# Other written-out orders for both phases of a fused scan and local-attention kernel

## The chip, the cores and the metric

One Trainium2 chip, one of its cores. The metric is the device time of one execution in microseconds (us). Two numbers are compared: the time before the change and the time after it, each the median of several runs.

## The reference, cut to what matters

Sixteen sequences of 512 tokens of width 256 pass through two blocks, each behind a layer norm, a modulation by a condition vector and a gated residual. The first is a selective scan (512 channels, 16 states each), the second two layers of windowed attention with a gated feed-forward part.

```python
h = _layernorm(x) * (1 + ca) + sa
xz = einsum(h, W_in);  x_ssm, z = split(xz)
dt = softplus(x_ssm @ W_dt + b_dt);  B_mat, C_mat = x_ssm @ W_B, x_ssm @ W_C
# for each token: h = exp(dt * A) * h + dt * B * x;  y = sum over states of h * C
y = (y + x_ssm * D) * silu(z)
x = x + ga * (y @ W_out)
h = _layernorm(x) * (1 + cb) + sb
for l in range(2):                       # 8 heads of 64, windows of 128 tokens
    q, k, v = split(shift_token(h) @ wqkv[l])
    q, k = rotary_xpos(l2norm(q) * qs, l2norm(k) * ksc)
    h = h + local_attention(q, k, v) @ wo[l]
    a, g = split(layernorm(shift_token(h)) @ w1[l] + b1[l])
    h = h + (a * gelu(g)) @ w2[l] + b2[l]
x = x + gb * h
```

## The kernel before, in words

The kernel runs two phases one after the other, `mixer_pass` (the scan block) and `stack_pass` (the two attention layers). Each is a software pipeline written in the same way. The work of one sequence is cut into named steps, such as `scan:7`. One long string, `MIXER_ORDER` (L139 to L160) or `ORDER` (L829 to L838), lists all steps of one pass, and every engine executes those steps of the list that it has a part in, in the order of the list, once per pass. The engines meet only at semaphores, so what matters is the order on each engine, not where a step of one engine stands against one of another. Each step has a lead, the sequence that it works on against the number of the pass; a "-" behind the name lowers it by one, a "+" raises it by one. So a pass holds work of three sequences. The scan phase works through 16 sequences, the second phase through 32 (16 in each of two layers), each with a filling pass ahead and a draining one behind.

**Scan phase.** The 512 channels x 16 states of a sequence are 32 units of 128 channels x 2 states x 512 tokens. Of unit q, `bcast:q` (TensorE, L565) spreads B over the partitions into one of two PSUM slots, `mul:q` (VectorE, L737) multiplies it by the step's input u, `decay:q` (ScalarE, L684) computes the decays, `scan:q` (VectorE, L755) runs the recurrence, `cmul:q` (GpSimd, L813) multiplies by C, and `sum:q` (TensorE, L573) adds the states up in PSUM. For ten of the units `mul` is GpSimd's (L806) and the decays go into the PSUM slot. `gate:d` (VectorE, L761) closes a chunk of 128 channels; gate 2 needs sums 0 to 30 and gate 3 sum 31. The slot of `bcast:q` is free when `scan:q-2` is done. `dtadd` (GpSimd, L792, L796) makes u for half of the channels. Decays, the rows of C and of B that are loaded from DRAM, and the states live in rings of 3, 2, 2 and 6 buffers (L33). A second set of TensorE steps makes the inputs of the next sequence: `xT`, `hT` (transposes), `xs`, `z`, `bc`, `dt` (projections, L524), and `out`, `mean2`, `var2` (L492) end the previous one.

**Second phase.** On TensorE: `pq`, `pk`, `v` (projections of one window of 128 tokens, L1296), `ptr` (transposes of rotated q and k, L1326), `score` (L1346), `pt` (transposes of the probabilities, L1357), `att` (L1373), `wo` (L1286), `mean`, `var`, `ga:0` to `ga:5` (the two halves g and a of the feed-forward part, 128 hidden columns each, 6 matmuls per half, L1407; `ga:5` has a g alone) and `wd:0` to `wd:5` (L1428). On ScalarE: `psq` (squares of q and k, L1459), `prate` (L1466, L1468), `exp` (eight heads, L1506), `gelu` (L1557), `hh` (L1571), `ptc` (copy of the transposed q out of PSUM, L1474), `dev`, `hn` and copies. On VectorE: `pss` (L1669, L1673), `pnorm` (L1680), `prot` (by sine, L1695), `padd` (L1701), `mask` (L1728, L1734), `rate` (L1745), `gated` (L1802), `hns` (cuts the normalised tokens in two parts for TensorE, L1650, L1652). On GpSimd: `prot` (by cosine, L1601), `pn` (L1628), `hl` (L1635).

A string `BANK_OF` gives each product of TensorE one of the eight PSUM banks; before a product starts, TensorE waits until the bank's last product has been read (`Banks.wait_free`). The bank of g0 to g4 is read out by `gelu`, that of a0 to a4 by `gated`, of q_t by `ptc` on ScalarE. ScalarE changes its function table between `gelu` and the exponentials, so a `gelu` that is followed by an `exp`, `prate` or `dev` in the list has a table load behind it (`LAST_GELUS`), and the next `gelu` one ahead of it. Squares of q and k are written to the buffer `qk_rot`, which later takes the rotated ones; `square_qk` waits for the sums of the squares of the window before, and since TensorE's order has `ptr:w-1` ahead of `pq:w`, the transposes have read the buffer by then.

Of the kernel before, what the change touches and what calls it, by code (L numbers as in the profile page):

```python
# [32 lines left out]
DECAY_SLOTS, STATE_SLOTS, C_SLOTS, B_SLOTS = 3, 6, 2, 2  # L33
# [106 lines left out]
sum-:5 bcast-:10 sum-:6 mul-:12 mul-:13 xload:0 bcast-:11 scan-:12 cload-:13 cload-:14 cload-:15 scan-:13 cload:0  # L140
cload:1 bload:6 sum-:7 cmul-:10 cload:2 mul-:14 sum-:8 cload:3 decay-:18 bcmid-:0 xs-:0 cmul-:11 cmul-:12 cmul-:13
cmul-:14 xscopy-:3 cload:4 decay-:19 cload:5 bcast-:12 sum-:9 decay-:20 xs-:1 xs-:2 decay-:21 mul-:15 scan-:14
scan-:15 mul-:16 cload:6 scan-:16 bload:9 mul-:17 bcast-:13 bcrest-:0 decay-:22 cmul-:15 mul-:18 soft-:0 scan-:17
decay-:23 bcast-:14 bcast-:15 mul-:19 cload:7 cload:8 gate-:0 bclow-:0 gate-:1 cmul-:16 cmul-:17 decay-:24 zcopy-:0
cmul-:18 cmul-:19 cmul-:20 decay-:25 sum-:10 zcopy-:1 cstore:0 sum-:11 bc-:0 bcast-:16 scan-:18 zcopy-:2 decay-:26
decay-:27 cload:9 sum-:12 zcopy-:3 decay-:28 bload:12 scan-:19 bcast-:17 cload:10 decay-:29 cmul-:21 sum-:13 mul-:20
mul-:21 soft-:1 scan-:20 xs-:3 sum-:14 bcast-:18 scan-:21 decay-:30 mul-:22 mul-:23 sum-:15 mul-:24 mul-:25 dt-:0
cmul-:22 decay-:31 scan-:22 bcast-:19 bcast-:20 decay:0 skip-:1 scan-:23 decay:1 stat:0 cload:11 bcast-:21
scan-:24 sum-:16 sum-:17 cmul-:23 bcast-:22 sum-:18 bcast-:23 decay:2 sum-:19 scan-:25 decay:3 cmul-:24 sum-:20
sum-:21 mul-:26 mul-:27 dtadd-:0 z-:0 scan-:26 decay:4 bcast-:24 scan-:27 x1store:0 silu-:0 z-:1 mul-:28 decay:5  # L150
cload:12 bcast-:25 z-:2 mul-:29 bcast-:26 z-:3 scan-:28 cmul-:25 cmul-:26 cmul-:27 norm:0 cmul-:28 cmul-:29 bcast-:27
h2store:0 sum-:22 dt-:1 cmul-:30 bcast-:28 scan-:29 sum-:23 bcast-:29 mul-:30 sum-:24 mul-:31 sum-:25 xcopy:0 decay:6
# [710 lines left out]
def stack_pass(nc, inp, mod, x1_dram, stack_dram, parts_dram, rotary_dram, out):  # L863
# [5 lines left out]
    with ExitStack() as ctx:  # L869
# [17 lines left out]
        mask = squares[:, 2:4, :].rearrange("p a b -> p (a b)")  # L887
# [565 lines left out]
        def _(act):  # L1453
            def square_qk(s, slot, layer, w):
                for i, stem in enumerate("qk"):
                    psum.wait_full(act, s, f"{stem}{w}")
                    if i == 0:
                        act.wait_ge(qk_sum_done.sem, qk_sum_done.at(s, w))
# [187 lines left out]
        def _(dve):  # L1646
# [38 lines left out]
            def times_sin(s, slot, layer, w):  # L1685
# [3 lines left out]
                if s == 0:  # L1689
                    dve.wait_ge(rotary_done, 1)  # L1690
# [347 lines left out]
```

## Time and profile before

| what | value |
|---|---|
| time, median of 3 runs | 4316.37 us (4315.1 to 4318.74) |
| the profiled execution's own time | 4316.54 us |
| its span | 4314.5 us |
| TensorE (PE) busy | 4052.9 us, 94% |
| VectorE (DVE) busy | 3679.9 us, 85% |
| ScalarE (ACT) busy | 2672.4 us, 62% |
| GpSimd (POOL) busy | 2639.3 us, 61% |
| granted TensorE clock, mean | 0.981 |

The scan phase fills the first 1.74 ms of the span, the second phase the rest. The page gives shares over the whole span; since the two phases have different limits, each has to be read from its own stretch. PE is TensorE's matmuls, PEld its weight loads, which run beside them. A line "A <- B: t, n" of the waits says that A stood idle for t us in n waits, which B ended.

### The profile page before, as it was taken

What the parts mean: (1) busy time and instruction counts of PE and PEld (TensorE: products, weight loads), DVE (VectorE), ACT (ScalarE), POOL (GpSimd) and SP (SyncE); (2) the same over time, 40 slices, a digit from 0 to 9 for tenths busy, and PEclk for the clock granted to TensorE, in tenths of its full rate; (3) what the DMA queues carried; (4) which work ended last, traced back from release to release, by engine and by line L of the source; (5) the groups of instructions that cost most, each with busy time, mean ns of one, the idle gap of its engine ahead of it and who ended that gap; (6) DMA issues with size and microseconds to landing.
All of it is one profiled execution on the core that took longest, in us unless ns stands there. A gap on an engine that the chain in (4) does not pass through costs nothing.

```text
span 4314.5 us, 60081 instructions
## 1 busy us (share of the span) xinstructions
PE 4052.9 (94%) x19614; PEld 2629.3 (61%) x19614; DVE 3679.9 (85%) x5981; ACT 2672.4 (62%) x5767; POOL 2639.3 (61%) x1297
## 2 busy tenths in 40 slices
PE   7999999999999999659999999999999999999997
PEld 4444444444444444347777777777777777777775
DVE  4999999999999999668888788888888888888873
ACT  5666666666666665335656565665656566565654
POOL 3999999999999999553434434343434334343432
PEclk8999999999999999879999999999999999999998
DMA  2333333333333333421000000001010100101000
GB/s 96 108 118 121 123 120 118 118 118 119 122 118 118 121 121 112 144 78 35 16 27 19 26 21 25 21 17 63 29 68 21 35 26 27 33 25 35 20 30 25
DMA packets 118499, 295.02 MB, mean 68 GB/s; under 512 B 21208, under 2 KB 43664, under 8 KB 118192
## 3 DMA queue, kind: packets, MB, share of 16 engines
q1 hardware_dynamic: 116320, 291.15, 20.2%
q8 instruction: 160, 2.62, 0.3%
q14 instruction: 147, 1.20, 0.1%
q10 hardware_dynamic: 1872, 0.05, 0.0%
HBM read 248.52 MB, written 42.64 MB: 67 GB/s over the span
## 4 chain that ended last, share of the span: by engine, by line
PE 34%; DVE 14%; issue 4%; ACT 4%; DMA 1%; SPq 0%; POOL 0%; DVEq 0%; ACTq 0%
PE b_bank L1407 12%; PE b_bank L1428 6%; PE b_bank L1296 5%; PE b_bank L1357 3%; PE b_bank L1373 3%; PE b_bank L1286 3%; ACT b_scores L1506 2%; DVE b_scores L1728 2%; DVE b_qk L1680 2%; DVE b_qk_rate L1669 2%; PE b_bank L1326 1%; PE b_bank L1346 1%; DVE b_qk_rot L1695 1%; DVE b_qk_rot L1701 1%; DVE b_xc L1785 1%
## 5 line engine op out<-in xcount | busy, mean ns | idle before, releaser
L813 POOL TENSOR_TENSOR a_state<-a_state,a_c_wide 128x1024 f32<-128x1024 f32 x512 | 1196.0, 2369 | 37.4 <-DVE a_state L755 37.4
L1628 POOL TENSOR_TENSOR b_scores<-b_scores,b_row_rate 128x1024 f32<-128x1024 f32 (+1 forms) x256 | 426.5, 1682 | 969.6 <-DVE b_row_rate L1745 969.6
L573 PE MATMUL a_y_sum<-a_state,a_ident 128*128 128x512 f32 x2048 | 942.3, 598 | 0.7 <-POOL a_state L813 0.6
L755 DVE TENSOR_TENSOR_SCAN a_state<-a_decay,a_slot 128x1024 f32<-128x1024 f32 x352 | 788.9, 2271 | 1.9 <-ACT a_decay L684 0.6
L1296 PE MATMUL b_bank<-b_w_qkv,b_hx_part 128*128 128x512 f32 x2304 | 661.7, 426 | 35.2 <-DVE b_w_qkv L1830 16.2
L1506 ACT ACTIVATE b_scores<-b_scores,b_row_bias 128x256 f32<-128x256 f32 (+1 forms) x1024 | 478.0, 469 | 269.9 <-DVE b_row_bias L1734 269.9
L573 PEld LDWEIGHTS a_y_sum<-a_state,a_ident 128*128 128x128 f32 x2048 | 387.1, 191 | 401.0 <-issue 342.4
L684 ACT ACTIVATE a_decay<-a_dt,a_neg_a 128x512 f32<-128x512 f32 x704 | 458.8, 711 | 164.0 <-DVE a_state L755 163.8
L1407 PE MATMUL b_bank<-b_hn_part,b_w 128*128 128x512 f32 x2112 | 515.4, 399 | 25.6 <-DVE b_hn_part L1652 25.6
L1296 PEld LDWEIGHTS b_bank<-b_w_qkv,b_hx_part 128*128 128x128 f32 x2304 | 424.0, 193 | 157.7 <-issue 48.2
L1601 POOL TENSOR_TENSOR b_by_cos<-b_qk,b_rotary 128x1024 f32<-128x1024 f32 x128 | 336.7, 2631 | 252.0 <-DVE b_qk L1680 249.9
L1407 PEld LDWEIGHTS b_bank<-b_hn_part,b_w 128*128 128x128 f32 x2112 | 397.4, 189 | 134.4 <-DVE b_hn_part L1652 40.8
L737 DVE TENSOR_TENSOR a_slot<-a_u,a_slot 128x1024 f32<-128x1024 f32 x352 | 417.2, 1213 | 24.6 <-PE a_slot L565 24.5
L806 POOL TENSOR_TENSOR a_state<-a_u,a_b_wide 128x1024 f32<-128x1024 f32 x160 | 375.9, 2369 | 27.6 <-PE a_y_sum L573 26.4
L684 ACT ACTIVATE a_slot<-a_dt,a_neg_a 128x512 f32<-128x512 f32 x320 | 208.0, 682 | 273.1 <-DVE a_state L755 272.4
L1635 POOL TENSOR_TENSOR b_h_part<-b_h,b_h_part 128x512 fp32r<-128x512 f32 x160 | 205.2, 1291 | 267.9 <-ACT b_h_part L1571 267.9
L755 DVE TENSOR_TENSOR_SCAN a_state<-a_slot,a_state 128x1024 f32<-128x1024 f32 x160 | 357.9, 2269 | 6.7 <-ACT a_slot L684 6.4
L1728 DVE CUSTOM_DVE_ANT_0 b_scores<-b_bank,b_squares 128x256 f32<-128x256 f32 (+1 forms) x1024 | 337.5, 385 | 3.4 <-issue 3.4
L1428 PE MATMUL b_bank<-b_h_part,b_w 128*128 128x512 f32 x1088 | 296.2, 406 | 0.0
L1802 DVE SCALAR_TENSOR_TENSOR b_h<-b_bank,b_b_1a,b_gelu 128x512 f32<-128x512 f32 x192 | 143.4, 747 | 167.5 <-POOL b_h_part L1635 64.3
L565 PE MATMUL a_slot<-a_bc_parts,a_picks 96*128 96x512 bf16 x704 | 213.4, 386 | 69.0 <-DVE a_state L755 67.6
L1357 PE MATMUL b_bank<-b_squares,b_scores 128*128 128x128 f32 x1792 | 265.2, 277 | 12.3 <-DVE b_qk L1680 7.9
(201 smaller groups left out, 6859.4 us busy)
## 6 DMA issues: line engine op xcount, KB each, us to landing
a_c_wide<-bc_rows SPq DMA_DIRECT2D x256, 512.0 KB, 3.7
a_b_wide<-bc_rows SPq DMA_DIRECT2D x80, 512.0 KB, 4.8
b_hx<-stack_rows SPq DMA_DIRECT2D x64, 256.0 KB, 3.6
b_x_res<-stack_rows SPq DMA_DIRECT2D x32, 512.0 KB, 3.3
a_xt<-in_L_attn_x SPq DMA_DIRECT2D x16, 512.0 KB, 6.2
x_rows<-a_x_t SPq DMA_DIRECT2D x16, 512.0 KB, 5.3
stack_rows<-a_h_t SPq DMA_DIRECT2D x16, 512.0 KB, 5.3
stack_rows<-b_xc SPq DMA_DIRECT2D x16, 512.0 KB, 2.6
```

Of the source, the lines that this page charges most:

```text
L573: last = nc.tensor.matmul(y_sum[dd][:], ident[:], state[state_ring.slot[q]][:, i, :], start=False, stop=(j == GROUPS - 1 and i == GROUP - 1))
L684: last = nc.scalar.activation(to[:, i, :], dt[slot][:, d, :], ACT.Exp, scale=neg_a[:, d, n:n + 1])
L737: nc.vector.tensor_tensor(slots[q % 2][:], u[slot][:, d, :].unsqueeze(1).to_broadcast([P, GROUP, SEQ]), slots[q % 2][:], ALU.mult).then_in ...
L755: nc.vector.tensor_tensor_scan(flat(h), flat(factor), flat(term), 0.0, ALU.mult, ALU.add).then_inc(scan_done.sem, 1)
L813: nc.gpsimd.tensor_tensor(h[:], h[:], c_wide[c_ring.slot[q // 2]][:], ALU.mult).then_inc(cmul_done.sem, 1)
L1296: last = nc.tensor.matmul(psum.tile(name)[:], x[:, c, w * P:(w + 1) * P].bitcast(F32R), weights[:, c, cols:cols + INNER].bitcast(F32R), st ...
L1357: last = nc.tensor.transpose(psum.tile(name)[:, n * P:(n + 1) * P], scores[w % 2][:, h, blk * WINDOW:(blk + 1) * WINDOW], ident)
L1407: last = nc.tensor.matmul(psum.tile(f"{stem}{m}")[:], weights[:, c, at * P:(at + 1) * P].bitcast(F32R), x[:, c, :].bitcast(F32R), start=(n ...
L1428: last = nc.tensor.matmul(psum.tile(f"wd{m}")[:], weights[:, k, m * P:(m + 1) * P].bitcast(F32R), x[:, held, :].bitcast(F32R), start=(k == ...
L1506: e = nc.scalar.activation(scores[w % 2][:, h, lo:hi], scores[w % 2][:, h, lo:hi], ACT.Exp, bias=row_bias[:, w, h:h + 1], accum_out=row_su ...
L1628: nc.gpsimd.tensor_tensor(probs, probs, row_rate[:, w, at].unsqueeze(2).to_broadcast([P, 4, hi - lo]), ALU.mult)\
L1728: last = nc.vector.tensor_tensor_reduce(out=scores[w % 2][:, head, lo:hi], in0=psum.tile(f"s{w}_{g}_{h}")[:, at + lo:at + hi], in1=mask[:, ...
```

## The change

The change replaces both order strings and the table of banks, enlarges three rings of the scan phase (decays 3 to 4, rows of C 2 to 3, rows of B 2 to 3), and puts the squares of q and k into the buffer `qk` of the normalised ones. For this `square_qk` waits for both readers of `qk` in the window before, `times_sin` waits until the transposes of the window before have read `qk_rot`, and `normalise_qk` loses a wait. Every step is there as often as before. The diff, with the scan phase's string cut to the lines around the end of a sequence:

```diff
-DECAY_SLOTS, STATE_SLOTS, C_SLOTS, B_SLOTS = 3, 6, 2, 2
+DECAY_SLOTS, STATE_SLOTS, C_SLOTS, B_SLOTS = 4, 6, 3, 3
...
-cload:12 bcast-:25 z-:2 mul-:29 bcast-:26 z-:3 scan-:28 cmul-:25 cmul-:26 cmul-:27 norm:0 cmul-:28 cmul-:29 bcast-:27
-bcast-:30 scan-:30 bcast-:31 sq2:0 sum-:26 sum-:27 scan-:31 bload+:1 mul:0 sum-:28 decay:7 mul:1 bcast:0 bcast:1
-sum-:29 dev2:0 cmul-:31 decay:8 bcast:2 gate-:2 scan:0 mul:2 gate-:3 scan:1 xcopy:1 scan:2 scan:3 decay:9
-mul:3 mul:4 res:0 sum-:30 mod:0 cmul:0 scan:4 sum-:31 skip:0 decay:10 out:0 bcast:3 res:1 cmul:1 bcast:4 mul:5 out:1
-sum:1 cmul:5 mul:7 scan:6 bcast:7 mul:8 scan:7 xn2:0 decay:13 bload+:4 scan:8 xscopy:0 sum:2 decay:14 decay:15
-decay:16 xscopy:1 h2:0 scan:9 mul:9 xscopy:2 bcast:8 cmul:6 var2:0 bccopy:0 mul:10 xT:1 hcut:0 mul:11 cmul:7 cmul:8
...
+mul-:27 cmul-:27 scan-:26 scan-:27 decay:8 sum-:24 bcast-:29 mul-:28 sum-:25 mul-:29 sum-:26 bcast-:30 mod:1 up:1
+sum-:27 scan-:28 bcast-:31 cload:7 scan-:29 dt-:1 mul-:30 sum-:28 cload:8 bcast:0 dtadd-:0 sum-:29 bcast:1 mul-:31
+sum-:30 decay:9 cmul-:28 scan-:30 cload:9 scan-:31 cmul-:29 sum-:31 bload:12 decay:10 decay:11 cmul-:30 dev2:0 mul:0
+skip:0 scan:0 mul:1 xcopy:1 out:0 bcast:2 gate-:2 gate-:3 xscopy:0 scan:1 decay:12 bcast:3 cload:10 scan:2 h2store:0
+cmul-:31 scan:3 sum:0 mul:2 res:0 bcast:4 bcast:5 out:1 mul:3 decay:13 cmul:0 sum:1 mul:4 cmul:1 h2:0 mean2:0 mul:5
+bcast:6 xscopy:1 decay:14 dtadd-:1 cmul:2 cmul:3 scan:4 decay:15 xT:0 cstore:0 bcast:7 bcast:8 res:1 scan:5 cen2:0
...
-ptr-:3 mask:0.0 mask:0.1 att-:3 score:0.0 exp:0 pn:0.0 hxs:0 hxload:0 psq:0 score:0.1 score:1.0 wo:0 mask:1.0 add:0
-prate:0 rate:0 pss:0 pnorm:0 pq:0 pk:0 pn:0.1 resload:0 score:1.1 mask:1.1 add:1 prot:0 score:2.0 exp:1 padd:0 wo:1
-pn:1.0 rate:1 v:0 pt:0.0 pt:0.1 cen:0 vc:0 ptc:0 sq:0 psq:1 mean:0 pk:1 ptr:0 pn:1.1 mask:2.0 sqs:0 pq:1 pt:1.0 v:1
-prate:1 pss:1 pt:1.1 vc:1 dev:0 pnorm:1 var:0 mask:2.1 score:2.1 pt:1.2 v:2 pt:1.3 pk:2 prot:1 xn:0 att:0 onorm:0
-att:1 padd:1 mask:3.0 score:3.0 vc:2 hn:0 exp:2 hns:0 gelu:0 score:3.1 onorm:1 psq:2 mask:3.1 ptr:1 gated:0 rate:2
-pq:2 ga:0 pn:2.0 pss:2 ga:1 ptc:1 pn:2.1 hh:0 gated:1 gelu:1 prate:2 hl:0 pnorm:2 ga:2 ga:3 exp:3 gelu:2 pt:2.0 prot:2
-gated:2 pk:3 gated:3 hh:1 gated:4 ga:4 padd:2 hh:2 rate:3 pt:2.1 wd:0 x1load:0 gelu:3 gelu:4 hh:3 gelu:5 gated:5 ga:5
-ptc:2 ptr:2 pss:3 outstore:0 psq:3 pq:3 wd:1 pt:2.2 hl:1 wd:2 hh:4 prate:3 pnorm:3 hl:2 hl:3 pn:3.0 hh:5 hl:4 pt:2.3
-wd:3 pt:3.0 wd:4 hl:5 vc:3 pn:3.1 pt:3.1 fin:0 fin:1 wd:5 pt:3.2 prot:3 sum:0 sum:1 turnc:0 padd:3 pt:3.3 turnc:1
-onorm:2 ptc:3 v:3 store:0 att:2 turn:0 turn:1 onorm:3
+ptc-:3 pn:0.1 ptr-:3 pt-:3.2 pt-:3.3 score:0.0 mask:0.0 score:0.1 mask:0.1 att-:3 onorm-:3 hxs:0 hxload:0 exp:0
+score:1.0 mask:1.0 psq:0 prate:0 rate:0 wo:0 pq:0 pk:0 add:0 pss:0 pnorm:0 pt:0.0 pk:1 pt:0.1 resload:0 vc:0 mask:1.1
+prot:0 pn:1.0 padd:0 v:0 score:1.1 exp:1 add:1 score:2.0 wo:1 rate:1 ptr:0 psq:1 pq:1 ptc:0 store:0 sq:0 prate:1 vc:1
+mask:2.0 mean:0 cen:0 pss:1 sqs:0 v:1 pt:1.0 v:2 pnorm:1 pn:1.1 pt:1.1 dev:0 var:0 score:2.1 mask:2.1 pt:1.2 pt:1.3
+xn:0 onorm:0 prot:1 onorm:1 padd:1 vc:2 hn:0 gelu:0 x1load:0 pk:2 mask:3.0 pn:2.0 exp:2 att:0 hns:0 att:1 psq:2 ptc:1
+score:3.0 score:3.1 prate:2 mask:3.1 pk:3 ptr:1 pq:2 rate:2 pss:2 hl:0 gated:0 pnorm:2 hh:0 ga:0 exp:3 pn:2.1 ga:1
+gelu:1 prot:2 ga:2 gelu:2 gelu:3 ga:3 gated:1 hh:1 pt:2.0 hl:1 hl:2 gated:2 hl:3 ga:4 gated:3 gelu:4 rate:3 pt:2.1
+hh:2 wd:0 padd:2 pn:3.0 hh:3 ga:5 gated:4 hl:4 gelu:5 wd:1 outstore:0 hh:4 gated:5 ptc:2 ptr:2 pss:3 pq:3 hl:5 psq:3
+wd:2 pnorm:3 hh:5 pt:2.2 wd:3 pt:2.3 fin:0 wd:4 prate:3 fin:1 wd:5 pt:3.0 turnc:0 turnc:1 vc:3 v:3 att:2 pn:3.1 prot:3
+sum:0 sum:1 pn+:0.0 turn:0 padd:3 onorm:2 turn:1 pt:3.1
 BANK_OF = """
-q_t3:4 k_t3:5 wo0:5 s0_0_0:1 s0_0_1:5 s0_1_0:0 s0_1_1:2 wo1:7 s1_0_0:6 s1_0_1:7 q0:2 k0:6 s1_1_0:3 s1_1_1:4 pt0_0:4
-v0:1 mean:3 pt0_1:7 v1:4 s2_0_0:5 s2_0_1:0 s2_1_0:7 s2_1_1:2 k1:6 var:0 q_t0:2 k_t0:4 q1:1 pt1_0:2 pt1_1:5 pt1_2:5
-v2:3 pt1_3:6 s3_0_0:5 s3_0_1:4 k2:7 s3_1_0:6 s3_1_1:3 o0:3 o1:0 q_t1:2 k_t1:1 q2:5 k3:7 pt2_0:5 pt2_1:6 pt2_2:6
-pt2_3:1 g0:4 a0:0 g1:3 a1:2 g2:4 a2:6 g3:0 a3:2 g4:1 a4:3 wd0:4 wd1:5 g5:1 q_t2:2 k_t2:3 q3:0 pt3_0:7 pt3_1:7 pt3_2:0
-pt3_3:3 o2:7 o3:6 v3:6 y0:5 y1:2
+q_t3:2 k_t3:7 wo0:2 s0_0_0:3 s0_0_1:2 s0_1_0:7 s0_1_1:4 wo1:7 s1_0_0:7 s1_0_1:3 q0:5 k0:4 s1_1_0:3 s1_1_1:5 pt0_0:0
+v0:1 mean:5 pt0_1:7 v1:7 s2_0_0:0 s2_0_1:1 s2_1_0:3 s2_1_1:7 k1:2 var:5 q_t0:3 k_t0:6 q1:4 pt1_0:0 pt1_1:1 pt1_2:0
+v2:6 pt1_3:4 s3_0_0:7 s3_0_1:5 k2:1 s3_1_0:4 s3_1_1:2 o0:0 o1:3 q_t1:3 k_t1:5 q2:7 k3:6 pt2_0:4 pt2_1:4 pt2_2:4
+pt2_3:2 g0:0 a0:5 g1:0 a1:2 g2:3 a2:5 g3:7 a3:1 g4:0 a4:5 wd0:0 wd1:3 g5:7 q_t2:1 k_t2:4 q3:7 pt3_0:6 pt3_1:0 pt3_2:5
+pt3_3:6 o2:7 o3:6 v3:4 y0:5 y1:6
...
-        qk_sq = qk_rot
+        qk_sq = qk
-                        act.wait_ge(qk_sum_done.sem, qk_sum_done.at(s, w))
+                        act.wait_ge(by_cos_done.sem, by_cos_done.at(s, w))
+                        act.wait_ge(by_sin_done.sem, by_sin_done.at(s, 2 * w))
-                dve.wait_ge(by_cos_done.sem, by_cos_done.at(s, w))
+                dve.wait_ge(k_t_full.sem, k_t_full.at(s, w))
```

Read engine by engine, the strings differ in these places, among others. Only steps of the engine named are shown, with "|" where a pass ends.

```
scan phase, VectorE   before: scan-:30 scan-:31 mul:0 mul:1 gate-:2 scan:0 gate-:3 scan:1 scan:2 scan:3
                      after:  scan-:30 scan-:31 mul:0 scan:0 mul:1 gate-:2 gate-:3 scan:1 scan:2 scan:3
scan phase, TensorE   before: z-:3 bcast-:27 sum-:22 dt-:1 bcast-:28 sum-:23 bcast-:29 sum-:24 sum-:25 bcast-:30
                              bcast-:31 sum-:26 sum-:27 sum-:28 bcast:0 bcast:1 sum-:29 sum-:30 sum-:31 skip:0 out:0
                      after:  z-:3 bcast-:27 sum-:22 sum-:23 bcast-:28 sum-:24 bcast-:29 sum-:25 sum-:26 bcast-:30
                              sum-:27 bcast-:31 dt-:1 sum-:28 bcast:0 sum-:29 bcast:1 sum-:30 sum-:31 skip:0 out:0
                      before: bcast:7 sum:2 var2:0 xT:1 sum:3 sum:4 hT:0 hT:1 |
                      after:  bcast:7 sum:2 hT:0 sum:3 hT:1 sum:4 sum:5 var2:0 bcast:10 sum:6 bcast:11 sum:7 | xT-:1
second phase, ScalarE before: dev:0 pt:1.2 vc:2 hn:0 exp:2 gelu:0 psq:2 ptc:1 hh:0 gelu:1 prate:2 exp:3 gelu:2
                      after:  dev:0 pt:1.2 vc:2 hn:0 gelu:0 exp:2 psq:2 ptc:1 prate:2 hh:0 exp:3 gelu:1 gelu:2
second phase, TensorE before: pk:2 att:0 att:1 score:3.0 score:3.1 ptr:1 pq:2 ga:0 ga:1 ga:2 ga:3 pt:2.0 pk:3 ga:4
                      after:  pk:2 att:0 att:1 score:3.0 score:3.1 pk:3 ptr:1 pq:2 ga:0 ga:1 ga:2 ga:3 pt:2.0 ga:4
second phase, VectorE before: mask:3.0 hns:0 onorm:1 mask:3.1 gated:0 rate:2 pss:2 ptc:1 gated:1 pnorm:2
                      after:  mask:3.0 hns:0 ptc:1 mask:3.1 rate:2 pss:2 gated:0 pnorm:2 prot:2 gated:1
```

## Rows read from the trace of the kernel before

**Rows 1.** By stretch: start:end, length, busy us (instructions) per engine, TensorE clock, DMA share, GB/s.
```profile
500.00:606.28 106.28, 100.15 (x300) 48.80 (x299) 103.64 (x67) 73.66 (x126) 102.78 (x48) 1.00 0.37 120
...
2508.28:2582.61 74.33, 73.53 (x457) 55.77 (x457) 61.36 (x152) 45.37 (x117) 30.02 (x17) 1.00 0.06 22
```
**Rows 2.** All waits of VectorE, and one of GpSimd, from 500 to 1600 us.
```profile
DVE a_u L761 <- PE a_y_sum L573: 18.1, 10, 1.9
DVE a_slot L737 <- PE a_slot L565: 6.2, 12, 1.4
DVE a_state L755 <- ACT a_slot L684: 2.7, 10, 0.3
...
POOL a_state L806 <- PE a_y_sum L573: 19.3, 17, 1.5
```
**Rows 3.** Timeline from 594 to 612 us: start, us, engine, what [idle before it].
```profile
596.97 4.46 DVE L755 TENSOR_TENSOR_SCAN a_state<-a_decay,a_slot 128x1024 f32<-128x1024 f32 x2
...
601.34 2.33 DVE L737 TENSOR_TENSOR a_slot<-a_u,a_slot 128x1024 f32<-128x1024 f32 x2
...
601.48 0.60 PE L565 MATMUL a_slot<-a_bc_parts,a_picks 96*128 96x512 bf16 x2 [0.43 <-DVE a_state L755]
...
601.92 5.32 PE L573 MATMUL a_y_sum<-a_state,a_ident 128*128 128x512 f32 x12
...
605.56 0.69 DVE L761 TENSOR_TENSOR a_u<-a_y_sum,a_sz 128x512 f32<-128x512 f32 x1 [1.89 <-PE a_y_sum L573]
```
**Rows 4.** TensorE's timeline in the second phase, from ga:0 on, one pass.
```profile
2582.61 11.46 PE L1407 MATMUL b_bank<-b_hn_part,b_w 128*128 128x512 f32 x48 [0.54 <-DVE b_hn_part L1652]
2593.90 0.60 PE L1357 MATMUL b_bank<-b_squares,b_scores 128*128 128x128 f32 x4
2594.26 1.63 PE L1296 MATMUL b_bank<-b_w_qkv,b_hx_part 128*128 128x512 f32 x6
```
**Rows 5.** ScalarE's timeline over the same stretch, exp:2 first.
```profile
2579.03 0.49 ACT L1506 ACTIVATE b_scores<-b_scores,b_row_bias 128x256 f32<-128x256 f32 x1
...
2583.07 1.28 ACT L1557 ACT_TABLE_LOAD   x1
2584.37 0.69 ACT L1557 ACTIVATE b_gelu<-b_bank,b_b_1g 128x512 f32<-128x512 f32 x1
2584.95 1.08 ACT L1459 ACTIVATE b_qk_rot<-b_bank 128x512 f32<-128x512 f32 x2
2585.91 0.61 ACT L1474 ACTIVATE b_q_t<-b_bank 128x512 f32<-128x512 f32 x1
2586.56 0.63 ACT L1571 ACTIVATE b_h_part<-b_h 128x512 fp32r<-128x512 f32 x1
2587.11 0.69 ACT L1557 ACTIVATE b_gelu<-b_bank,b_b_1g 128x512 f32<-128x512 f32 x1
2587.81 1.28 ACT L1560 ACT_TABLE_LOAD   x1
2589.11 0.22 ACT L1466 ACTIVATE b_qk_rate<-b_qk_rate 128x16 f32<-128x16 f32 x1
...
2589.57 0.49 ACT L1506 ACTIVATE b_scores<-b_scores,b_row_bias 128x256 f32<-128x256 f32 x1
```
**Rows 6.** VectorE's timeline over the same stretch.
```profile
2585.78 0.75 DVE L1802 SCALAR_TENSOR_TENSOR b_h<-b_bank,b_b_1a,b_gelu 128x512 f32<-128x512 f32 x1 [1.02 <-PE b_bank L1407]
...
2586.55 1.17 DVE L1669 TENSOR_REDUCE b_qk_rate<-b_qk_rot 128x16 f32<-128x1024 f32 x1
2587.75 0.88 DVE L1673 TENSOR_SCALAR b_qk_rate<-b_qk_rate 128x16 f32<-128x16 f32 x1
...
2606.81 0.17 DVE L1673 TENSOR_SCALAR b_qk_rate<-b_qk_rate 128x16 f32<-128x16 f32 x1
```
**Rows 7.** TensorE's timeline near the end of the span.
```profile
4224.84 13.02 PE L1407 MATMUL b_bank<-b_hn_part,b_w 128*128 128x512 f32 x48 [2.57 <-DVE b_hn_part L1652]
```
**Rows 8.** The same place by stretch, columns as in the first group.
```profile
4225.00:4232.00 7.00, 7.00 (x24) 5.54 (x25) 2.80 (x14) 3.52 (x5) 1.50 (x1) 0.76 0.00 0
```

More of the change, by code:

```diff
@@ L139 @@
 MIXER_ORDER = """
[L140 to L149, printed above, removed]
@@ L155 @@
-mul:3 mul:4 res:0 sum-:30 mod:0 cmul:0 scan:4 sum-:31 skip:0 decay:10 out:0 bcast:3 res:1 cmul:1 bcast:4 mul:5 out:1
-dtadd-:1 sum:0 bcast:5 up:0 cmul:2 scan:5 xT:0 bcast:6 mod:1 cen2:0 decay:11 up:1 cmul:3 cmul:4 mean2:0 decay:12 mul:6
-sum:1 cmul:5 mul:7 scan:6 bcast:7 mul:8 scan:7 xn2:0 decay:13 bload+:4 scan:8 xscopy:0 sum:2 decay:14 decay:15
-decay:16 xscopy:1 h2:0 scan:9 mul:9 xscopy:2 bcast:8 cmul:6 var2:0 bccopy:0 mul:10 xT:1 hcut:0 mul:11 cmul:7 cmul:8
-sum:3 cmul:9 sum:4 hcut:1 scan:10 scan:11 bcast:9 hT:0 decay:17 bcup:0 hT:1
+scan-:10 scan-:11 cmul-:6 cmul-:7 scan-:12 scan-:13 bcast-:13 bcmid-:0 xT-:1 xs-:0 xscopy-:3 xs-:1 decay-:19 soft-:0
@@ new lines @@
+cmul-:8 sum-:8 decay-:20 cmul-:9 decay-:21 mul-:12 mul-:13 mul-:14 xs-:2 decay-:22 cmul-:10 decay-:23 decay-:24
+bcast-:14 mul-:15 cmul-:11 cmul-:12 sum-:9 scan-:14 bcast-:15 sum-:10 bload:6 zcopy-:0 bc-:0 bcast-:16 decay-:25
+cload-:15 sum-:11 xload:0 scan-:15 decay-:26 zcopy-:1 bcast-:17 zcopy-:2 cmul-:13 mul-:16 bcrest-:0 cload:0 sum-:12
+cmul-:14 sum-:13 cload:1 decay-:27 sum-:14 decay-:28 bcast-:18 cmul-:15 mul-:17 mul-:18 cload:2 xs-:3 decay-:29
+bload:9 sum-:15 bcast-:19 dt-:0 zcopy-:3 bcast-:20 cload:3 mul-:19 scan-:16 cmul-:16 skip-:1 decay-:30 bcast-:21
@@ new lines @@
+scan-:17 gate-:0 bclow-:0 scan-:18 cload:4 decay-:31 sum-:16 decay:0 sum-:17 bcast-:22 gate-:1 silu-:0 sum-:18
+cmul-:17 cmul-:18 scan-:19 mul-:20 bcast-:23 mul-:21 scan-:20 decay:1 soft-:1 scan-:21 mul-:22 sum-:19 bcast-:24
+decay:2 sum-:20 bcast-:25 decay:3 cmul-:19 cmul-:20 cload:5 z-:0 z-:1 cmul-:21 mul-:23 decay:4 stat:0 mul-:24 mul-:25
+decay:5 decay:6 scan-:22 norm:0 cmul-:22 scan-:23 xcopy:0 cmul-:23 sq2:0 cmul-:24 cmul-:25 sum-:21 z-:2 cmul-:26
+x1store:0 bcast-:26 decay:7 z-:3 mod:0 bcast-:27 sum-:22 scan-:24 scan-:25 up:0 mul-:26 sum-:23 cload:6 bcast-:28
@@ L160 @@
+bcast:6 xscopy:1 decay:14 dtadd-:1 cmul:2 cmul:3 scan:4 decay:15 xT:0 cstore:0 bcast:7 bcast:8 res:1 scan:5 cen2:0
+cload:11 sum:2 cmul:4 hT:0 mul:6 sum:3 cload:12 hT:1 mul:7 scan:6 hcut:0 cmul:5 sum:4 scan:7 xscopy:2 bccopy:0
+bload+:1 sum:5 bload+:4 decay:16 bcast:9 var2:0 bcast:10 cload:13 scan:8 sum:6 mul:8 scan:9 mul:9 mul:10 xn2:0 mul:11
+hcut:1 decay:17 bcast:11 cload:14 sum:7 bcup:0 decay:18 bcast:12
 """
```

2 lines of the change are left out of this document (removed).

## The prediction

> **What bounds the kernel now.** Busy time by stretch first. In the scan phase one sequence takes 106.28 us and three engines are nearly full: VectorE is busy for 103.6 us of it, GpSimd for 102.8, TensorE for 100.2. In the second phase one sequence takes 74.33 us, TensorE is busy for 73.5 of it, VectorE for 61.4, ScalarE for 45.4 [rows 1]. So the scan phase is VectorE's, with at most 2.6 us to gain per sequence, and the second phase TensorE's, with at most 0.8. Both are short of their bound by waits alone, since no step is added or removed. The waits come second. VectorE's in ten sequences of the scan phase sum to 18.1 + 6.2 + 2.7 = 27 us, and two thirds of them are the gate's wait for a sum of states [rows 2]. In the second phase TensorE waits once per sequence, 0.54 us, for the cut of the normalised tokens ahead of ga:0 [rows 4]. The timeline comes last, to walk the new orders through with measured durations: an order of TensorE that is nearly free of gaps can be spoilt much more than it can be improved.
>
> **Scan phase: the gate.** Count from the end of scan:31, which the next multiplication follows at once (601.34) [rows 3]. Before, TensorE has bcast:1 next, which had to wait for just this scan (601.48), and only then sums 29, 30, 31: twelve matmuls in 5.3 us, so 1.7 to 1.8 us a sum. VectorE does two multiplications (2.33 us), then stands for 1.89 us until sum 30 is in [rows 3]. After, sum 29 lies before bcast:1. TensorE is through with sum 30 at about 0.1 + 0.6 + 1.8 = 2.5 us and with sum 31 at about 4.3 us if GpSimd keeps up, and VectorE has a scan (half of 4.46 us, [rows 3]) more to do ahead of the gate, so it comes there at 2.33 + 2.2 = 4.6 us. The 1.89 us go. What is late next: gate 3, at 5.2 us, needs sum 31 with less than 1 us to spare.
>
> **Scan phase: the rest.** The move of dt-:1 (12 matmuls) from in front of bcast-:28 and bcast-:29 to behind bcast-:31 takes it out of the way of a multiplication that waited for bcast-:29 (most of the 6.2 us in ten sequences); behind it stand only sum 28 and bcast:0, which are not late. GpSimd's wait of 1.5 us for sum 3 ahead of mul:9 (19.3 us in ten sequences, [rows 2]) goes too, since two steps (var2, xT:1) leave TensorE's way. On the other side hcut:0 now comes 2.8 us earlier on VectorE and needs a longer row of ScalarE's steps (sq2, a decay, mod, up), and dev2 now stands behind three more decays. I allow 0.9 us of new waits. Sum: 27 / 10 = 2.7 us of waits, 0.9 stays or is new, and GpSimd is full at 102.8 us: about 1.6 us less a sequence, bounds 2.6 (VectorE without a wait) and -1.0 (hcut and xn2 a microsecond late each, which would eat the gain and more). Over 15 steady sequences: -24 us, from -39 to +15.
>
> **Rings.** No wait for a DMA is among GpSimd's in the scan phase, and ScalarE's waits for free decay buffers lie in its idle third (73.7 us busy of 106.28) [rows 1, 2]. More buffers take away no wait that anybody waits for: 0 us. If the cover were gone, ScalarE would first lose its 32.6 idle us per sequence, and what is left would be inside the bounds above. The new order of SP's loads puts x1store and h2store between loads of C; both wait for steps of VectorE and ScalarE that are over before the ring has room for the next load. 0 us.
>
> **Buffer of the squares.** It costs nothing and gives nothing. In the new order, too, ptr:w-1 stands ahead of pq:w on TensorE, and ptr follows padd, which follows both products with cosine and sine. So when q is full, everything that square_qk and times_sin newly wait for is done. Above and below: a semaphore wait that is already met, a few hundredths of a us.
>
> **Second phase: gelu:0 ahead of exp:2.** This is the large term. Count from the first matmul of ga:0 (2582.61 before), and take ScalarE's row of steps. gelu:0 starts at 2584.37, 1.76 us after it, since it needs g0. Before, exp:2 was done by then (2579.03 to 2583.07) and psq:2 and ptc:1 followed at once [rows 5]. After, exp:2 stands behind gelu:0, though its scores are ready 3.6 us ahead of ga:0 at the latest (2579.03): gelu:0 and the table load that now follows it (2587.11 to 2587.81 to 2589.11: 0.70 + 1.30) end at 3.76; exp:2 takes 4.04 (2579.03 to 2583.07), to 7.80; psq:2 0.96, to 8.76; ptc:1 0.61, to 9.4 [rows 5]. The new table of banks gives g2 the bank of q_t1 (3), which ptc:1 reads out. TensorE comes to g2 after four products of six matmuls, 24 x 11.46 / 48 = 5.73 us [rows 4]. Everything else of TensorE is queued behind g2. It waits 3.7 us.
>
> **The second wait of the same pass.** a2 has the bank of a0, free after gated:0, which now stands behind pss:2: psq:2 ends at 8.76, the sum of squares takes 1.20 (2586.55 to 2587.75), the floor 0.17, gated:0 0.75, so 10.9; g2 ends at 10.8: 0.1 us. Then prate:2 (0.46, beside gated:0), hh:0 (0.55), exp:3 (4.04) and a table load (1.30) stand ahead of gelu:1: 10.9 + 0.6 + 4.0 + 1.3 = 16.8, and gelu:1 is through at 17.5 [rows 5, 6]. g4 has the bank of g1 (0), which gelu:1 reads. TensorE is through with g2 to a3 at 10.9 + 4.3 = 15.2 and with pt:2.0 (0.36) at 15.6, and waits 1.9 us. From there on gated:1 and gated:2 (0.75 each) end at 19.0, just when a4 needs its bank. Walking on to wd:5 I find no further wait. Sum: 5.7 us a sequence, in the 31 passes that have a gelu of one sequence beside the exponentials of the next.
>
> **What the second phase gives back.** The wait of 0.54 us at ga:0: VectorE now does prot:0 and padd:0 ahead of the residual (ahead of the chain to hns:0), while TensorE has one projection less between wo:1 and ga:0 (pk:1 and v:0 go ahead of wo:1, pk:3 comes in, 24 x 11.46 / 48 / 4 = 1.4 us each). By my walk hns:0 is then in time. I take 0.5 us; bounds 0.8 (all of TensorE's idle time) and -1.0 (another order of short products with more gaps between them). Sum of the phase: 31 x (5.7 - 0.5) = +161 us. Bounds: 31 x (3.7 - 0.8) = +90 if only the first wait stands on the path, 31 x (5.7 + 1.0) = +208.
>
> **Sum.** The profiled execution took 4316.54 us, 0.17 above the median of the runs. 4316.5 - 24 + 161 = 4453.5. Filling and draining passes and the weights' setup keep their work: 0, within 5 us either way.
>
> **Rivals.**
> (a) *The clock falls in the gaps.* Near the end of the span TensorE stood for 2.57 us, and the 48 matmuls behind it took 13.02 us in place of 11.46 [rows 4, 7]; the granted clock over these 7 us was 0.76, a part of it at 1.2 instead of 2.4 GHz [rows 8]. That is 1.56 us a fall. The first gap, 3.7 us, would slow g2 to a3, and the second wait absorbs that: it ends by ScalarE's row, not TensorE's. A fall in the second gap, 1.9 us, would be paid in full: 31 x 1.56 = 48, so 4502 us. For it: the 2.57 us gap. Against it: that one came after a stretch with many small gaps, and here 60 us of work without one come first. [...]
> (b) *Only the first wait is on the path*, because exp:3 and gelu:1 run beside TensorE's work better than I have it: 4316.5 - 24 + 31 x 3.2 = 4392 us.
> (c) *More waits behind*: VectorE loses some 10 us to waiting per sequence, 61.4 + 10 of 79.5 us. If its backlog makes one more product late by 2 us, 62 us: 4515 us.
> (d) *The other side.* ScalarE's row does not reach TensorE. The place is g2: it decides whether 9.4 us of ScalarE's row fit under what TensorE has to do between the start of ga:0 and g2. That is 5.73 us as I read the order; with another 3.7 us of work there, or if exp:2 ran ahead of gelu:0 in fact, nothing is lost and the phase gives its 0.5 us: 4316.5 - 24 - 16 = 4276 us. For it: TensorE reaches 99% in the kernel before with an order of the same kind. Against it: queues run in order, and every duration of the row is measured.
> (e) *The change does nothing*, because both gains and losses hide: within 0.2%, about 8.6 us, which is what a measurement here can tell from no change.
>
> **How the numbers follow.** Forecast 0.50, (a) 0.15, (b) 0.13, (c) 0.10, (d) 0.10, (e) 0.02. The forecast's own range is 4425 to 4480. The range of 4375 to 4525 takes in (a), (b) and the smaller half of (c). Faster 0.10, within 0.2% 0.02, slower 0.88.
>
> **What would show it.** The second phase's sequence takes about 79.5 us against 74.33. Ahead of one g product in the middle of ga TensorE stands for 3.7 us, released by ScalarE's copy of q_t, and ahead of g4 for 1.9 us, released by gelu. exp:2 starts 3.8 us after ga:0, not before it. In the scan phase the sequence takes 104.7 us, and the gate's wait of 1.9 us is gone. TensorE's share in the second phase falls to some 93%. I am wrong if these waits are absent or end by another engine, or if the scan phase's sequence is above 106.28 us.

## The result and the profile after

The changed kernel takes 4413.35 us (median of 4 runs, 4411.63 to 4415.54), the one before in the same session 4316.72 us (4315.1 to 4318.74). The ratio is 1.0224, interval 1.0206 to 1.0242: 97 us slower. The profiled execution took 4411.63 us, its span is 4409.8 us.

The two phases went in opposite directions. From the start of the span to the first product ga:0 it is 1941.60 us in place of 1987.82, so the scan phase gave 46.2 us. (Before, VectorE still runs a scan at 1767 us, so the scan phase fills a little more than the 1.74 ms named ahead of the prediction.) From there to the end it is 2468.2 us in place of 2326.7, so the second phase lost 141.5 us.

Busy time by stretch, one steady sequence of each phase after, the counterpart of [rows 1] (us of the stretch, then busy us and count of TensorE, weight loads, VectorE, ScalarE and GpSimd, granted clock, DMA share, GB/s):
```profile
500.00:603.66 103.66, 100.09 (x300) 48.96 (x299) 103.33 (x67) 73.57 (x126) 102.72 (x47) 1.00 0.37 123
2573.94:2652.83 78.89, 73.80 (x457) 55.86 (x456) 58.75 (x152) 46.22 (x116) 30.27 (x17) 1.00 0.06 21
```
The scan sequence is 103.66 us and VectorE is busy for 103.33 of it: it waits for next to nothing now. The second phase's sequence is 78.89 us in place of 74.33, and TensorE's busy time has hardly moved (73.80, before 73.53). What was added is waiting. In the second of the two layers a sequence takes 0.9 us more both before and after (75.25 and 79.76 us); over the 29 steady passes of both layers the change adds 131.7 us, 4.54 a pass.

VectorE's and GpSimd's waits from 500 to 1600 us, the counterpart of [rows 2] (us in total, times, longest):
```profile
DVE a_slot L737 <- PE a_slot L565: 2.3, 10, 0.2
POOL a_state L813 <- DVE a_state L755: 5.6, 10, 0.6
POOL a_state L806 <- PE a_y_sum L573: 2.5, 11, 0.2
```
The 18.1 us for the gate and 2.7 us for decays have gone, and 6.2 have become 2.3.

TensorE's timeline over one pass of the second phase, the counterpart of [rows 4] (start, us, engine, what, [idle before it and who ended it]; the edit to the buffers moved the line numbers by one):
```profile
2573.94 5.76 PE L1407 MATMUL b_bank<-b_hn_part,b_w 128*128 128x512 f32 x24
2583.09 6.10 PE L1407 MATMUL b_bank<-b_hn_part,b_w 128*128 128x512 f32 x24 [3.38 <-ACT b_q_t L1475]
2589.02 0.60 PE L1357 MATMUL b_bank<-b_squares,b_scores 128*128 128x128 f32 x4
2591.33 3.10 PE L1407 MATMUL b_bank<-b_hn_part,b_w 128*128 128x512 f32 x12 [1.71 <-ACT b_gelu L1558]
```
ga:0 starts without a wait. After 24 matmuls TensorE stands at g2 for 3.38 us until ScalarE has copied q_t, and at g4 for 1.71 us until gelu:1 is through, 17.39 us after the start of ga:0. In between there is a third, short wait that the merged rows do not show as idle: the first matmul of a2 starts 0.37 us behind the one ahead of it (2584.72 against 2584.35), where its neighbours follow at 0.23 us. It comes 0.05 us after gated:0, which reads out the bank that a2 is to have, is through on VectorE:
```profile
2583.92 0.75 DVE L1803 SCALAR_TENSOR_TENSOR b_h<-b_bank,b_b_1a,b_gelu 128x512 f32<-128x512 f32 x1
```
That is 0.14 us. After the waits at g2 and a2 the second matmul follows the first one at 0.34 us, not 0.23. These two starts (0.1 us each) and the 0.14 us are the 0.34 us by which the 24 matmuls behind g2's wait take longer than the 24 ahead of it (6.10 and 5.76).

ScalarE over the same stretch, the counterpart of [rows 5]:
```profile
2575.54 0.69 ACT L1558 ACTIVATE b_gelu<-b_bank,b_b_1g 128x512 f32<-128x512 f32 x1 [6.13 <-PE b_bank L1407]
2576.25 1.28 ACT L1561 ACT_TABLE_LOAD   x1
2577.55 0.51 ACT L1507 ACTIVATE b_scores<-b_scores,b_row_bias 128x256 f32<-128x256 f32 x1
...
2581.50 1.05 ACT L1460 ACTIVATE b_qk<-b_bank 128x512 f32<-128x512 f32 x2
2582.45 0.58 ACT L1475 ACTIVATE b_q_t<-b_bank 128x512 f32<-128x512 f32 x1
...
2589.30 1.28 ACT L1558 ACT_TABLE_LOAD   x1
2590.59 1.27 ACT L1558 ACTIVATE b_gelu<-b_bank,b_b_1g 128x512 f32<-128x512 f32 x2
```
This is the row of the prediction: ScalarE stands for 6.13 us ahead of gelu:0, since the exponentials that were ready are queued behind it. exp:2 starts 3.61 us after ga:0 and the copy of q_t ends at 9.09; g2 starts at 9.15.

The passes are not all alike. The same place two passes earlier, TensorE's timeline:
```profile
2424.52 7.32 PE L1407 MATMUL b_bank<-b_hn_part,b_w 128*128 128x512 f32 x24 [3.39 <-ACT b_q_t L1475]
2432.76 3.11 PE L1407 MATMUL b_bank<-b_hn_part,b_w 128*128 128x512 f32 x12 [0.48 <-ACT b_gelu L1558]
```
And by stretch, columns as above (the value after the five engines is the granted clock), the 24 matmuls in this pass, in the one shown first, and in the pass between:
```profile
2424.52:2432.02 7.50, 7.50 (x28) 6.01 (x28) 6.38 (x7) 6.38 (x20) 5.89 (x4) 0.78 0.00 0
2583.09:2589.09 6.00, 6.00 (x25) 4.55 (x26) 5.93 (x7) 4.91 (x18) 4.39 (x4) 1.00 0.00 0
2503.78:2512.28 8.50, 8.49 (x26) 6.71 (x27) 6.67 (x8) 7.37 (x22) 6.89 (x4) 0.65 0.01 3
```
The wait at g2 comes in 30 passes. In 26 of them the 24 matmuls behind it take 7.2 to 8.7 us, and the granted clock is below 1.00: a part of them ran at 1.2 in place of 2.4 GHz. In the other four they take 6.10 us. Most of the passes with a fall (at 7.4 to 7.5 us) are no longer than one at 6.10, since the wait at g4 is shorter by as much (0.39 in place of 1.71): both take 78.89 us. In the pass shown with 7.32 us g4, too, starts 17.38 us after ga:0, as in the one with 6.10; the pass is 79.26 us long by a wait of 0.30 us for VectorE 66 us behind ga:0, which e11 below has in its seventh pass as well. Only a pass at 8.5 us, where g4 does not wait at all, is 0.4 us longer (79.30).

### The profile page after: what moved, and what is told of

Its sections match the earlier page's. It is cut to its first block, busy times and chain, and to the rows that moved or that the text cites. A ratio compares the mean times of both kernels' runs of the same rounds, so it can differ in the third digit from the quotient of the medians.

```text
span 4409.8 us, 60202 instructions
## 1 busy us (share of the span) xinstructions
PE 4088.7 (93%) x19614; PEld 2664.2 (60%) x19614; DVE 3594.0 (81%) x5981; ACT 2694.7 (61%) x5767; POOL 2645.6 (60%) x1297
## 4 chain that ended last, share of the span: by engine, by line
PE 47%; ACT 9%; DVE 3%; issue 1%; DMA 0%; POOL 0%; SPq 0%; DVEq 0%; ACTq 0%
PE b_bank L1296 12%; PE b_bank L1428 6%; PE b_bank L1407 6%; PE b_bank L1286 5%; PE b_bank L1346 5%; PE b_bank L1373 5%; ACT b_scores L1507 5%; PE b_bank L1357 4%; PE b_bank L1326 3%; DVE b_qk_rate L1670 1%; ACT L1561 1%; ACT b_gelu L1558 1%; PE b_bank L1392 1%; ACT b_qk L1460 1%; ACT L1558 1%
## 5 line engine op out<-in xcount | busy, mean ns | idle before, releaser
L1629 POOL TENSOR_TENSOR b_scores<-b_scores,b_row_rate 128x1024 f32<-128x1024 f32 (+1 forms) x256 | 442.2, 1738 | 1091.1 <-DVE b_row_rate L1746 1091.1
L1407 PE MATMUL b_bank<-b_hn_part,b_w 128*128 128x512 f32 x2112 | 571.1, 427 | 127.3 <-ACT b_q_t L1475 101.4
L1296 PE MATMUL b_bank<-b_w_qkv,b_hx_part 128*128 128x512 f32 x2304 | 650.7, 421 | 20.2 <-DVE b_w_qkv L1831 16.2
L1407 PEld LDWEIGHTS b_bank<-b_hn_part,b_w 128*128 128x128 f32 x2112 | 425.6, 205 | 256.3 <-ACT b_q_t L1475 114.4
L1602 POOL TENSOR_TENSOR b_by_cos<-b_qk,b_rotary 128x1024 f32<-128x1024 f32 x128 | 321.3, 2510 | 346.1 <-DVE b_qk L1680 344.0
L1670 DVE TENSOR_REDUCE b_qk_rate<-b_qk 128x16 f32<-128x1024 f32 x128 | 155.9, 1218 | 178.3 <-ACT b_qk L1460 178.2
L1428 PE MATMUL b_bank<-b_h_part,b_w 128*128 128x512 f32 x1088 | 286.5, 402 | 0.0
L1558 ACT ACTIVATE b_gelu<-b_bank,b_b_1g 128x512 f32<-128x512 f32 x192 | 128.7, 687 | 228.9 <-PE b_bank L1407 220.3
```

Of the source, the lines that this page charges most:

```text
L1296: last = nc.tensor.matmul(psum.tile(name)[:], x[:, c, w * P:(w + 1) * P].bitcast(F32R), weights[:, c, cols:cols + INNER].bitcast(F32R), st ...
L1407: last = nc.tensor.matmul(psum.tile(f"{stem}{m}")[:], weights[:, c, at * P:(at + 1) * P].bitcast(F32R), x[:, c, :].bitcast(F32R), start=(n ...
L1428: last = nc.tensor.matmul(psum.tile(f"wd{m}")[:], weights[:, k, m * P:(m + 1) * P].bitcast(F32R), x[:, held, :].bitcast(F32R), start=(k == ...
L1629: nc.gpsimd.tensor_tensor(probs, probs, row_rate[:, w, at].unsqueeze(2).to_broadcast([P, 4, hi - lo]), ALU.mult)\
```

## The experiments

Twelve kernels, timed against the kernel before, whose median in the three sessions was 4315.42, 4315.86 and 4314.56 us. "After" with an edit means the changed kernel with that edit.

**Each half alone.** *e1_scan_alone*: the kernel before with the new scan-phase order and the new rings.
```
-MIXER_ORDER = (before)        DECAY_SLOTS, ... = 3, 6, 2, 2
+MIXER_ORDER = (after)         DECAY_SLOTS, ... = 4, 6, 3, 3
```


> The changed kernel's scan phase (order and rings) with the second phase of before. Theory (the two phases are independent, and the scan phase gives what the traces show between the start of the span and the first ga:0, 46 us): 4316.7 - 46 = 4271 us. Rival (the scan phase's gain is partly an earlier start of the second phase under its own order, so the old second phase gives some back): 4285 us or more. In the profile: a sequence of the scan phase takes 103.7 us, one of the second phase 74.3 us.

Measured: 4275.06 us, ratio 0.9904 (0.9888 to 0.9921), 40 us faster. *e2_stack_alone* is the other half: the new ORDER, BANK_OF and squares' buffer with the old scan phase.

> The second phase of the changed kernel (order, banks, buffer of the squares) with the scan phase of before. Theory (independent phases, second phase 141 us longer by the traces): 4316.7 + 141 = 4458 us. Rival (part of the loss is made by the scan phase's end, whose order changed too): 4440 us or less. In the profile: a sequence of the scan phase takes 106.3 us, one of the second phase 78.9 us, with waits of 3.4 us ahead of g2 and 1.7 or 0.4 us ahead of g4.

Measured: 4458.52 us, ratio 1.033 (1.0314 to 1.0345), 143 us slower, with the same two waits (84.5 us in 25 passes at g2, 14.1 in 21 at g4, between 2100 and 4100 us). -40 + 143 = +103 us, the change +97: the halves are nearly independent.

**The step that the prediction names.** *e3_exp2_first*: after, with one word of ORDER moved.
```
-xn:0 onorm:0 ... vc:2 hn:0 gelu:0 x1load:0 pk:2 mask:3.0 pn:2.0 exp:2 att:0
+xn:0 onorm:0 ... vc:2 hn:0 exp:2 gelu:0 x1load:0 pk:2 mask:3.0 pn:2.0 att:0
```


> The changed kernel with one step of ScalarE moved: exp:2 ahead of gelu:0. Theory (ScalarE's row from ga:0 to gelu:1 sets the time, and exp:2 is 4.04 us of it): ptc:1 is over at 5.3 us, before TensorE comes to g2 at 5.7, so the wait of 3.4 us goes; gelu:1 comes at 17.4 - 4.0 = 13.4 us, TensorE at g4 at 11.8, so a wait of 1.5 us stays there. Per sequence 78.9 - 4.0 = 74.9 us, 31 times: 4413 - 125 = 4288 us. Rival (the wait at g2 is the only cost and the one at g4 a sequel of the slow clock, so it goes with it): 4413 - 31 x 4.6 = 4270 us. Rival 2 (TensorE waits for something else at g2, as the cut of the normalised tokens): no gain, 4413 us.

Measured: 4291.98 us, ratio 0.9946 (0.9931 to 0.9961): 121 us back from one step. TensorE's timeline in one pass:
```profile
2542.26 11.36 PE L1407 MATMUL b_bank<-b_hn_part,b_w 128*128 128x512 f32 x48
2555.72 3.11 PE L1407 MATMUL b_bank<-b_hn_part,b_w 128*128 128x512 f32 x12 [1.67 <-ACT b_gelu L1558]
```
The first wait is gone, the second stands. The sequence takes 74.98 us, 3.9 less than after.

**ScalarE's whole row.** *e10_rows_before*: e3 with gelu:1 and the gating steps placed as before too.
```
 exp:2 ahead of gelu:0 (as in e3)
+hh:0 gelu:1 ahead of prate:2 and exp:3;  gated:0 ahead of rate:2;  gated:1 ahead of pnorm:2
```


> The changed kernel with ScalarE's row and VectorE's row between ga:0 and gelu:2 in the order of before: exp:2 gelu:0 psq:2 ptc:1 hh:0 gelu:1 prate:2 exp:3 gelu:2, and gated:0 ahead of rate:2, gated:1 ahead of pnorm:2. Theory (these two rows are the whole loss): no wait at g2, and gelu:1 early enough for g4; a4 has the bank of a2, which gated:2 reads at about 13.7 us, TensorE comes at 13.3: 0.4 us left. Second phase as before or a little shorter, so 4271 us, 4262 to 4280. Rival (the rest of the new order or the new banks cost something too): above 4285 us.

Measured: 4255.98 us, ratio 0.9862 (0.9847 to 0.9876), 15 us below my value and below its range. A sequence takes 73.87 us, less than the 74.35 of before, although one wait is left:
```profile
PE b_bank L1407 <- DVE b_h L1803: 16.4, 27, 0.6
```
That is a4, which waits for the bank of a2. *e11_rows_and_bank* gives a4 the bank of a1.
```
-g4:0 a4:5
+g4:0 a4:2
```


> This is the kernel after with ScalarE's row and the gating steps in the order of before (exp:2, gelu:0, psq:2, ptc:1, hh:0, gelu:1, prate:2, exp:3, and gated:0 and gated:1 earlier), and with product a4 in the bank of a1 instead of the bank of a2. In the run without the bank change one wait is left per sequence, 0.61 us ahead of a4, released by gated:2, and a sequence takes 73.87 us. My theory: the rest of the new order leaves TensorE without any wait, so the bank alone takes the 0.61 us away: 73.3 us a sequence, 4256 - 31 x 0.6 = 4238 us. Rival: the time is set by something that runs in parallel with TensorE (VectorE's row), and the wait turns up at another product: 4256 us.

Measured: 4246.96 us (4244.09 to 4247.29), ratio 0.9837 (0.982 to 0.9855). The bank took the wait away, but gave 0.5 us a sequence (73.37), so the time is 9 us above my value; some 4 us of these lie ahead of the second phase (first ga:0 at 1945.75 us, 1941.58 in e10). Between 2100 and 4100 us TensorE has no wait above 0.3 us left. This kernel beats both: 69 us below the one before, 166 below the changed one.

**Was it the bank?** *e5_bank_g2*: after, g2 in a bank that is free earlier.
```
-pt2_0:4 ... g2:3
+pt2_0:3 ... g2:4
```


> This is the kernel after with g2 in bank 4 instead of bank 3, so that it does not wait for ScalarE's copy of q_t; pt2.0 takes bank 3. My theory: ScalarE's row is what is late, not the bank. TensorE then gets one product further and waits for gated:0 ahead of a2 until about 10.8 us after the start of ga:0, and g4 waits for gelu:1 as before, until 17.4: the time stays at 4413 us within 5, with the first wait named by gated:0. Rival: the bank is the cause, and the first wait goes: 4413 - 31 x 3.4 = 4308 us.

Measured: 4419.67 us, ratio 1.0239 (1.0223 to 1.0256), 6 us above the changed kernel, where I had said within 5; its first ga:0 comes at 1946.12 us, 4.5 us later than in the changed kernel's trace, though its scan phase is the same. TensorE, one pass:
```profile
2815.80 7.17 PE L1407 MATMUL b_bank<-b_hn_part,b_w 128*128 128x512 f32 x30
2826.59 4.46 PE L1407 MATMUL b_bank<-b_hn_part,b_w 128*128 128x512 f32 x18 [3.62 <-DVE b_h L1803]
2833.20 3.11 PE L1407 MATMUL b_bank<-b_hn_part,b_w 128*128 128x512 f32 x12 [1.71 <-ACT b_gelu L1558]
```
One product more, and then the wait is for gated:0, which VectorE does behind the sum of the squares of ScalarE's late row. The bank only chose where TensorE stopped. (2826.59 to 2833.20 is a pass at full clock.)

**What a fall of the clock costs.** Two kernels. *e12_no_second* was to keep the first gap and take the second wait away.
```
-score:3.1 prate:2 ... exp:3 pn:2.1 ga:1 gelu:1 prot:2          a4:5
+score:3.1 gelu:1 prate:2 ... exp:3 pn:2.1 ga:1 prot:2          a4:2
```


> This is the kernel after with gelu:1 right behind ptc:1 on ScalarE (ahead of prate:2 and exp:3), and a4 in the bank of a1. The wait of 3.4 us ahead of g2 stays as it is, and the second wait (1.7 us ahead of g4) has nothing left to wait for. In the kernel after, the 24 matmuls behind the first wait take 7.4 us in most passes in place of 5.7, and the second wait is shorter by the same amount. My theory: the second wait paid for these slow matmuls, and without it they are paid in full: 74.98 - 1.69 (the run with exp:2 first, without its wait) + 3.38 + 1.7 = 78.4 us a sequence, some 4398 us. Rival: the slow matmuls are slow because there is time, or the clock does not fall here: 73.3 + 3.4 + 0.4 = 77.1 us a sequence, 4358 us. Either fails if gelu:2, which now stands two table loads further behind, makes another product late: then a new wait named by gelu or gated:2 appears and the time stays at 4413 or above.

Measured: 4444.66 us, ratio 1.0301 (1.0282 to 1.0319): neither theory, but the third case of the text, except that the new waits are named by the normalisation and by a copy of probabilities, not by gelu or gated:2. TensorE's timeline in a pass without a fall:
```profile
2590.35 3.31 PE L1407 MATMUL b_bank<-b_hn_part,b_w 128*128 128x512 f32 x12 [3.37 <-ACT b_q_t L1475]
2594.94 3.07 PE L1407 MATMUL b_bank<-b_hn_part,b_w 128*128 128x512 f32 x12 [1.28 <-DVE b_qk L1680]
2598.20 3.08 PE L1407 MATMUL b_bank<-b_hn_part,b_w 128*128 128x512 f32 x12
2602.26 0.66 PE L1357 MATMUL b_bank<-b_squares,b_scores 128*128 128x128 f32 x4 [0.97 <-ACT b_probs_t L1519]
```
The second, with the fall:
```profile
3229.39 7.65 PE L1407 MATMUL b_bank<-b_hn_part,b_w 128*128 128x512 f32 x24 [3.37 <-ACT b_q_t L1475]
...
3237.24 3.25 PE L1407 MATMUL b_bank<-b_hn_part,b_w 128*128 128x512 f32 x12
```
prate:2, now behind two more table loads, made VectorE's normalisation late, and with it g3; exp:3, late too, held up ScalarE's copy of the turned probabilities. g4 starts 7.85 us after g2 in both passes. So again a wait absorbed the fall, and the fall's own price stayed open.

*e13_one_gap* gets it. It is e11 with ScalarE's copy of q_t for window 1 moved behind prate:2 and cut into eight pieces.
```
 def rate_qk(s, slot, layer, w): ...
+    if w == 2: copy_q(s, slot, layer, 1, late=True)
 def copy_q(s, slot, layer, w, late=False):
+    if w == 1 and not late: return
+    (for w == 1: eight ACT.Copy of 64 columns each, the signal on the last)
```


> This is the kernel without any wait in the second phase (rows of before, a4 in the bank of a1; 4247 us) with one gap put in by hand: ScalarE copies q_t of window 1 only after prate:2, in eight pieces, so that g2 waits for its bank for about 3 us. ScalarE and VectorE have time left behind it, so no second wait should follow. It prices one gap of the size seen in the kernel after. My theory: the clock falls in the gap in most passes and, as nothing behind it waits, the slow matmuls are paid in full: gap 3.0 + 1.7 = 4.7 us a sequence, 4247 + 31 x 4.7 = 4393 us, and passes without a fall are shorter by about 1.5 us than passes with one. Rival: only the gap itself counts: 31 x 3.0 = 93, so 4340 us, with all passes of one length.

Measured: 4326.51 us, ratio 1.0028 (1.0017 to 1.0039), 80 us above e11. Neither number came (4393 and 4340): the gap came out at 2.15 us, not 3.0, and the clock fell in fewer than half of the passes. No wait follows the gap. TensorE's timeline at g2 in three passes, one with a fall and the next two without:
```profile
2180.43 7.41 PE L1407 MATMUL b_bank<-b_hn_part,b_w 128*128 128x512 f32 x24 [2.15 <-ACT b_q_t L1483]
...
2257.36 5.86 PE L1407 MATMUL b_bank<-b_hn_part,b_w 128*128 128x512 f32 x24 [2.16 <-ACT b_q_t L1483]
...
2332.81 5.87 PE L1407 MATMUL b_bank<-b_hn_part,b_w 128*128 128x512 f32 x24 [2.15 <-ACT b_q_t L1483]
```
The stretches behind the first two of these gaps, with their granted clock:
```profile
2180.43:2188.34 7.91, 7.91 (x29) 6.37 (x30) 5.13 (x4) 7.05 (x21) 4.38 (x3) 0.78 0.00 0
2257.36:2265.27 7.91, 7.91 (x36) 6.45 (x37) 5.16 (x4) 7.56 (x22) 4.79 (x3) 1.00 0.01 2
```
From g2 to the next pass's g2 it is 76.93 us with the fall and 75.45 without: 1.5 us, all of it paid. It fell in 13 of 30 passes. 30 x 2.15 + 13 x 1.5 = 84 us, measured 80. So rival (a)'s mechanism is real at its price of 1.56 us, where nothing behind the gap waits; in the changed kernel g4's wait stands behind it.

**The squares' buffer.** *e6_squares_back*: after, with `qk_sq = qk_rot` and the waits of before.

> This is the kernel after with the squares of queries and keys written to the buffer of the rotated ones again, with the waits of before. My theory: the buffer costs and gives nothing, 4413 us within 4. Rival: the new waits of square_qk (for both products with cosine and sine) hold back psq:2 and are a part of the first wait: then it gains up to 31 x 1 us, 4382 us.

Measured: 4415.66 us, ratio 1.0234 (1.0219 to 1.0249), beside 4413.35: no change.

**The rings.** *e7_rings_3623*: after, with three decay buffers and two of C.
```
-DECAY_SLOTS, STATE_SLOTS, C_SLOTS, B_SLOTS = 4, 6, 3, 3
+DECAY_SLOTS, STATE_SLOTS, C_SLOTS, B_SLOTS = 3, 6, 2, 3
```


> This is the kernel after with three decay buffers in place of four and two buffers of C in place of three, as before; the ring of B keeps its third buffer, which the new order needs. My theory: the rings give nothing, since ScalarE has a third of its time idle in the scan phase: 4413 us within 5. Rival: the new order takes its speed from the rings (decays and loads run further ahead), and without them VectorE waits for ScalarE's decays or GpSimd for C: 1 to 2.6 us a sequence, up to 4455 us.

Measured: 4452.98 us, ratio 1.0319 (1.0301 to 1.0336), 40 us above the changed kernel. The rival holds. A scan sequence takes 106.11 us (before 106.28, and 107.4 in three of 15), nearly all that the new order had gained is gone. VectorE's waits from 500 to 1600 us, the row that is new:
```profile
DVE a_state L755 <- ACT a_slot L684: 25.7, 11, 2.3
```
One of them on VectorE's timeline:
```profile
713.56 4.47 DVE L755 TENSOR_TENSOR_SCAN a_state<-a_slot,a_state 128x1024 f32<-128x1024 f32 x2 [2.34 <-ACT a_slot L684]
```
And ScalarE's timeline ahead of it:
```profile
694.51 1.34 ACT L684 ACTIVATE a_decay<-a_dt,a_neg_a 128x512 f32<-128x512 f32 x2 [4.80 <-DVE a_state L755]
...
701.13 1.33 ACT L684 ACTIVATE a_decay<-a_dt,a_neg_a 128x512 f32<-128x512 f32 x2 [3.10 <-DVE a_state L755]
...
712.23 2.52 ACT L684 ACTIVATE a_slot<-a_dt,a_neg_a 128x512 f32<-128x512 f32 x4
```
ScalarE stands for 4.80 and 3.10 us until a scan frees a decay buffer, works off what is queued behind, and comes to the decay that VectorE needs next 2.34 us late. The wait names ScalarE, and ScalarE stood for a decay buffer, so it is that ring: from 500 to 1600 us the decays stand for 119.8 us until a scan frees a buffer, in the changed kernel for 70.1. The ring of C was cut in the same run, and its share was not taken by itself; GpSimd's waits in this trace are for VectorE (20.2 us) and TensorE (12.3), none for a load of C. The new rings in the order of before were not tried.

**What of the order made the scan phase faster?** *e9_gate_alone*: the kernel before with the gate edit only.
```
-mul:0 sum-:28 decay:7 mul:1 bcast:0 bcast:1 sum-:29 ... gate-:2 scan:0 mul:2 gate-:3 scan:1
+mul:0 sum-:28 decay:7 scan:0 mul:1 bcast:0 sum-:29 bcast:1 ... gate-:2 mul:2 gate-:3 scan:1
```


> This is the kernel before with one local edit of the scan phase: sum 29 goes ahead of bcast:1, scan:0 ahead of mul:1, and both gates ahead of scan:1. Nothing else of the change. My reading of the two traces: of the 2.6 us that a sequence of the scan phase became shorter, 1.9 are the gate's wait for a sum and 0.7 are the rest of the reordering. Then this kernel gains 1.9 x 16 = 30 us: 4287 us, and the scan phase's sequence takes 104.4 us. Rival: the gate's wait only moves to another place (the multiplication behind it, or bcast:0 and bcast:1, which now come later), and what gained was the move of the dt product: 4317 us, no change.

Measured: 4301.98 us, ratio 0.9966 (0.9954 to 0.9978), 14 us faster, half of my value. VectorE's waits from 500 to 1600 us:
```profile
DVE a_slot L737 <- PE a_slot L565: 13.0, 17, 1.4
DVE a_state L755 <- ACT a_slot L684: 2.7, 10, 0.3
DVE a_u L761 <- PE a_y_sum L573: 2.3, 7, 0.3
```
The gate's 18.1 us are 2.3, but the wait for broadcasts has grown from 6.2 to 13.0: sequences of 104.6 and of 106.3 us mixed. *e14_three_moves* has this edit too (left out below), and moves dt-:1 behind bcast-:31 and bcast:0 ahead of sum-:28.
```
-sum-:22 dt-:1 cmul-:30 bcast-:28 ... bcast-:31 sq2:0 ... mul:0 sum-:28 decay:7 mul:1 bcast:0
+sum-:22 cmul-:30 bcast-:28 ... bcast-:31 dt-:1 sq2:0 ... mul:0 bcast:0 sum-:28 decay:7 scan:0 mul:1
```


> This is the kernel before with three local edits of the scan phase: the gate edit (sum 29 ahead of bcast:1, scan:0 ahead of mul:1, both gates ahead of scan:1), dt-:1 behind bcast-:31 instead of ahead of bcast-:28, and bcast:0 ahead of sum-:28. The gate edit alone gained 14 us: the gate's wait of 1.9 us went, but in every other sequence VectorE waited 1.4 us for a broadcast instead. My theory: the scan phase is VectorE's row without waits, and these three places held most of them: 104.0 us a sequence, 4279 us. Rival: each local edit only moves the wait, and only the whole new order gets rid of it: 105.3 us a sequence, 4300 us.

Measured: 4401.6 us, ratio 1.0202 (1.0187 to 1.0217), 87 us slower, worse than the rival. One place, first on ScalarE's timeline:
```profile
726.95 0.69 ACT L667 ACTIVATE a_dt<-a_work,a_b_dt 128x512 f32<-128x512 f32 x1 [9.49 <-PE a_work L524]
...
730.63 2.56 ACT L684 ACTIVATE a_decay<-a_dt,a_neg_a 128x512 f32<-128x512 f32 x4
```
and then on VectorE's:
```profile
732.05 4.46 DVE L755 TENSOR_TENSOR_SCAN a_state<-a_decay,a_slot 128x1024 f32<-128x1024 f32 x2 [6.21 <-issue]
```
ScalarE's softplus waits 9.49 us for the moved product, the decays queued behind it come late, and VectorE stands for 6.21 us. The profile names nobody for this wait ("issue"); that it is for the decays is read from ScalarE's timeline, where they start only at 730.63. In the changed kernel the product has room: it starts 8.2 us ahead of its softplus. So these three moves are not enough; which further moves of the new order are needed was not tested.

## Why the prediction came out as it did

4453.5 us was forecast, 4413 came: right side, right mechanism, inside the range of 4375 to 4525, 40 us too high. Two terms were mis-sized, 22 and 20 us, both the same way, so nothing cancelled.

- **First wait, g2: 3.7 us said, 3.38 measured.** The place, the releaser and the row hold; gelu:0 started 1.60 us after ga:0 instead of 1.76, and the rest of ScalarE's row ran 0.15 us closer. e3 shows the cause: one step moved gives 121 us back.
- **Wait at a2: 0.1 said, 0.14 measured** in passes in which the clock does not fall before it (gated:0 is through at 10.73, said 10.9).
- **Second wait, g4: 1.9 said, 1.71 measured** where the clock did not fall; gelu:1 through at 17.39, said 17.5.
- **What the phase gives back: 0.5 said, 1.0 measured.** e11, with no wait left, takes 73.37 us, before 74.35. 0.55 of it is the wait at ga:0; the rest I had not counted. It is also why e10 fell 15 us below its value.
- **A cost that I had not named**: the first matmul behind a wait holds up the next by 0.1 us. Sum: 3.38 + 0.14 + 1.71, three times 0.1, less 1.0: 4.5 us a sequence, measured 78.89 - 74.35 = 4.54; said 5.2. Times 31: 141 us, measured 141.5; said 161. That 141 and 141.5 agree so well is in part chance: the 29 steady passes bring 131.7, and the last two passes and the end, which are of other lengths, 9.8.
- **The clock, rival (a).** The prediction said that the second wait would absorb a fall in the first gap, and it did. No fall was to be paid behind the second gap: e3 has that gap alone, and in all its 30 passes the 12 matmuls take 3.10 to 3.11 us and the granted clock behind the gap is 1.00; its sequences are 74.98. The Trainium skill, "TensorE: Matmul & The Clock Gate", section "Why this matters for your kernels", has it that idle gaps between bursts bring the half clock; the traces agree for the gap of 3.38 us (26 of 30 passes). That section of the Trainium skill names only gaps longer than those of 2.15 and 1.7 us: at 2.15 us the clock fell all the same, in 13 of 30 passes, and at 1.7 us it did not.
- **Rivals (b), (c), (d)** are out: both waits are there, TensorE's other waits, but for the short ones at a2, sum to 0.6 us from 2100 to 4100 us, and exp:2 did run behind gelu:0.
- **Scan phase: -24 said, -46 measured** (-40 in e1). I allowed 0.9 us of new waits and got none: 103.66 a sequence, said 104.7. The bound from VectorE's 103.64 busy us was the better estimate. My own terms, 2.7 - 0.9, give 1.8 us a sequence and 27 in all, where I wrote 1.6 and 24. From the first scan on the phase gave 40 us. The other 6 are its start: the first scan begins at 68.89 us in place of 74.97, where I had put 0. With the same scan phase it begins at 71.9 to 73.3 us in e1, e5, e6, e11 and e13, so 3 to 4 us of this are no gain that every execution shows.
- **Rings: 0 said, and this step failed.** The reason given was that ScalarE's waits for free decay buffers lie in its idle third. e7 shows that they do not: a queue that runs in order is late at the step behind a wait, however idle it is on average. That the term did not show in the sum is luck: I had taken the order's gain as if the rings were there. With three decay buffers and two of C the new order gains next to nothing in a steady sequence.
- **Gate: the wait went, for the reason given.** Alone it is worth 0.9 us a sequence, not 1.9 (e9), since the multiplication behind it waits for a broadcast instead.
- **Squares' buffer: 0 said, 0 measured** (e6).

## What to carry to other kernels

Walk each engine's queue in order with measured durations from the product that everybody waits for: the first step that is ready early but stands behind one that is not (exp:2 behind gelu:0) is where time goes, and here moving one word got 121 us back. An engine's idle share does not tell whether its waits cost; look at what stands behind the wait, and when it is needed. Once a place has such a late row, changing a bank only moves the stop (e5), and an edit that takes one wait away can move it or make a new one (e9, e12, e14; not e3 and e11).

## What the hardware showed that was not expected

A gap of 2.15 us, with no other wait above 0.35 us in its pass, was enough for the clock to fall in 13 of 30 passes (e13), one of 3.38 us in 26 of 30 (the changed kernel), and one of 1.7 us in none of 30 (e3); a fall cost 1.5 us where it was not covered. The passes do not scatter at random. In the changed kernel the 24 matmuls behind the gap take 8.57, 6.10, 7.50, 7.41, 7.41, 7.41 and 7.32 us in the first seven passes, and 8.53, 6.10, 7.50, 7.41, 7.42, 7.40 and 7.30 in the next seven; e2 and e6 have nearly the same row, which comes again after seven or eight passes. So the length of the gap does not decide alone; what else does was not tested. At a granted clock of 1.00, too, a wait costs a little more than its length: behind the waits of 1.7, 2.15 and 3.38 us, and even behind the 0.14 us at a2, the second matmul starts 0.34 us after the first, where the others follow at 0.23.
